# Macaron layer on one core: one more expert measured on ScalarE, four more tiles copied on GpSimd, and the order of all engines redrawn

## What is computed

```python
def ffn(x):                                  # 8 experts of 341 units, 4 chosen, one shared expert
    gate = x @ Wg.T + routing_bias
    weights = softmax(top_4_of(gate))
    out = swiglu(x, Ws1, Ws2, Ws3)           # sigmoid(h) * h * v, h = x @ W1.T, v = x @ W2.T
    for e in range(8):
        out += weights[..., e] * swiglu(x, W1[e], W2[e], W3[e])
    return out

x = x + 0.5 * ffn(layernorm(x))
x = x + attention(layernorm(x))              # 16 heads of 64, causal, 512 x 512 scores
x = x + 0.5 * ffn(layernorm(x))
```

## Time and profile before

| | us |
|---|---|
| time before, median of 3 runs (645.97 to 646.34) | 646.28 |
| time of the profiled execution | 646.15 |
| its span, first to last instruction | 644.4 |
| TensorE busy | 633.5 |
| VectorE busy | 593.0 |
| ScalarE busy | 557.1 |
| GpSimd busy | 506.0 |

### The profile page before, as it was taken

The page is one execution under the profiler, slowest core; times in us unless marked ns, Lnnn a source line. Parts: engine busy times, 40 slices in busy tenths (PEclk is TensorE's granted clock), DMA queues, the critical chain, the costliest instruction groups (busy, mean ns, idle before and its releaser), DMA issues.

```text
span 644.4 us, 21017 instructions
## 1 busy us (share of the span) xinstructions
PE 633.5 (98%) x7872; PEld 418.4 (65%) x7872; DVE 593.0 (92%) x1654; ACT 557.1 (86%) x1080; POOL 506.0 (79%) x633
## 2 busy tenths in 40 slices
PE   7899999999999999999999999999999999999998
PEld 5576655656676566667657666756666676766665
DVE  4999799999999999999999999999999998779887
ACT  4788997999999899999989999988999996475645
POOL 4476596789998878999877899969789997475555
PEclk9999999999999999999999999999999999999999
DMA  7900000689888376898755888863797695201000
GB/s 199 290 3 2 2 2 2 100 134 131 141 128 145 63 128 120 126 148 129 123 93 103 136 145 128 139 128 68 101 146 150 132 134 85 49 2 24 13 1 18
DMA packets 226489, 62.97 MB, mean 98 GB/s; under 512 B 213202, under 2 KB 225620, under 8 KB 226388
## 3 DMA queue, kind: packets, MB, share of 16 engines
q1 hardware_dynamic: 226388, 61.64, 55.9%
HBM read 7.87 MB, written 1.05 MB: 14 GB/s over the span
## 4 chain that ended last, share of the span: by engine, by line
PE 72%; DVE 18%; issue 4%; ACT 3%; SPq 1%; DMA 1%; DVEq 0%; ACTq 0%
PE bank L1197 21%; PE bank L1199 19%; PE bank L1198 19%; PE bank L1391 7%; DVE probs L1896 4%; PE bank L1354 4%; DVE glu L1800 4%; DVE xs L1835 3%; DVE glu L1805 2%; DVE vl L1611 1%; DVE ql L1611 1%; DVE kl L1611 1%; ACT glu L1534 1%; PE bank L1241 1%; DMA paired<-in_L_ffn_W 1%
## 5 line engine op out<-in xcount | busy, mean ns | idle before, releaser
L1160 POOL TENSOR_TENSOR glul<-glu,gluh 128x512 f16<-128x512 f32 x191 | 218.6, 1160 | 46.3 <-ACT gluh L1558 44.8
L1164 POOL TENSOR_TENSOR paired<-probs,paired 128x512 f16<-128x512 f32 x160 | 184.1, 1162 | 23.3 <-ACT paired L1583 22.6
L1537 ACT ACTIVATE glu<-bank,tanh_scale 128x512 f32<-128x512 f32 x167 | 112.4, 680 | 35.9 <-PE bank L1199 34.4
L1575 ACT ACTIVATE probs<-probs,exp_bias 128x128 f32<-128x128 f32 (+3 forms) x256 | 129.4, 553 | 2.7 <-POOL exp_bias L1172 2.6
L1896 DVE CUSTOM_DVE_ANT_0 probs<-bank,causal,score_scale 128x128 f32<-128x128 f32 (+3 forms) x256 | 126.2, 547 | 1.9 <-PE bank L1391 1.0
L1800 DVE SCALAR_TENSOR_TENSOR glu<-glu,bank 128x512 f32<-128x512 f32 x167 | 113.6, 680 | 11.8 <-ACT glu L1537 11.6
L1197 PE MATMUL bank<-w3h,gluh 128*128 128x128 f16 x696 | 122.1, 219 | 0.0
L1199 PE MATMUL bank<-w3h,glul 128*128 128x128 f16 x696 | 121.9, 219 | 0.0
L1198 PE MATMUL bank<-w3l,gluh 128*128 128x128 f16 x696 | 121.9, 219 | 0.0
L1805 DVE SCALAR_TENSOR_TENSOR glu<-glu,bank 128x512 f32<-128x512 f32 x167 | 114.7, 687 | 5.8
L1558 ACT ACTIVATE gluh<-glu 128x512 f16<-128x512 f32 x179 | 107.1, 621 | 13.2 <-DVE glu L1805 12.9
(11 more groups left out here) (228 smaller groups left out, 1621.9 us busy)
## 6 DMA issues: line engine op xcount, KB each, us to landing
pT<-paired SPq DMA_TRANSPOSE x160, 3.3
attention_raw<-in_L_attn_W_qkv SPq DMA_DIRECT2D x6, 256.0 KB, 5.1
xs<-in_L_attn_inputs SPq DMA_DIRECT2D x4, 256.0 KB, 4.6
vh<-in_L_ffn_W SPq DMA_DIRECT2D x6, 128.0 KB
pT<-in_L_ffn_W SPq DMA_DIRECT2D x6, 128.0 KB
out<-xs SPq DMA_DIRECT2D x3, 256.0 KB, 2.7
raw_more<-in_L_ffn_W SPq DMA_DIRECT2D x4, 128.0 KB
attention_raw<-in_L_attn_W_out SPq DMA_DIRECT2D x2, 256.0 KB, 6.1
```

The source lines that it names most:

```text
L1160: pool.tensor_tensor(glul[pair][:, :], g[:, :], gluh[pair][:, :], ALU.subtract).then_inc(glu_low)
L1164: pool.tensor_tensor(paired[n % PAIRED][:, 1, :], probs[n % PROBS][:, :], paired[n % PAIRED][:, 0, :], ALU.subtract).then_inc(probs_low)
L1537: act.activation(g[:, :], psum[b1.bank][:, :], ACT.Tanh, scale=tanh_scale[:, j:j + 1]).then_inc(tanh_made)
L1575: e = act.activation(pr[:, at:at + (qt + 1) * P], pr[:, at:at + (qt + 1) * P], ACT.Exp, bias=exp_bias[:, gp % 2, qt, head:head + 1], scale ...
```

## The change

Two constants and the four strings of `ORDER`. The steps, their banks and SyncE's queue are the same. Of the strings the diff shows the first line of two; all four are redrawn over their whole length.

```diff
-POOLED = 12
+POOLED = 16
 ...
-ADDED_BY = "VVAAAVVVA"
+ADDED_BY = "VVAAAAVVA"
...
     "tensor": (
-        "FFFFFTFFTBzTGNSgTTNhhGSTTTTTThTdhhddhhGddShdTTTddThhTTdddThGhhSTdTTdddhhRdTdhXhdzTTThdddhTgdhhhhhxdd"
+        "BFFFFTTzFFFTGNSgTTNhhGTTSTTTThTdhhddhhGdTSTTddTdhhhTdThdddGThShTThTddddhRdTTdXhhdzddTThhhTdhghhhdxdd"
...
     "scalar": (
-        "lCBzMMMNPPPPNMPhrhPPPhPPPPhhMMAhhhPPAAAhPPhMMMPAAhPhhsssssssssssssPPsAAAshPhsPPlhshszPPPhWQZshsPWWhh"
+        "lCBzMMMNPPPPPMhNrhPPPPhMPPPhhMAhhAAPPPAhAhhMMMhPPPhAhPhPAAAhPPPssssssssssssssssslhhWszPPPhWhhZPsWshh"
```

More of the change, by code:

```diff
@@ L715 @@
     "gpsimd": (
[L716 to L720, removed]
@@ L721 @@
-        "ssssssfsssssssssssssssssssssssH"
+        "LLnLLLLsfsssssLEELEsLsssssEssnssssWssWssssWWssnWssfYWssWWsssnssssbpbpbppsbppsbbppysbpsppbupsbpsbpppb"
+        "ubsspspppbsspbufbpppsbsppbuppbsspsbsppbnupbsppsbpypbubppsssppsssnsuusbypbpbsppbpppbbssppsbspppbbussp"
+        "spbppubsbppsppbsspbubppsspbpuppbbfspspbnppubpbsypsbpppsbusbspppssspssnsuubsyppbbpssbpspppbsbppbsppbu"
+        "bpspsspbppbubpsppfbsppubpbpspbsppubssbppssbpppbnupbspspbpyspbubppsnppsuysssssbsbupsbppfsbpppbsbppspp"
+        "bssppbbusspppbspbupbsppsbppbsbusppnbspppsbbuppsbspppupbbysspbpppbbssusppppssusssfssusssssnsssyssssss"
@@ L722 @@
+        "sssssssssssssfssssssssssssssssH"
     ),
     "tensor": (
-        "FFFFFTFFTBzTGNSgTTNhhGSTTTTTThTdhhddhhGddShdTTTddThhTTdddThGhhSTdTTdddhhRdTdhXhdzTTThdddhTgdhhhhhxdd"
-        "xdddhhhhhhddxhhxzdddkvvhhvvddhhqkhdqqvhdxqxkhddwwqqhwvhkqhwwwdddqqhwvhwqkwhwwddqqxvghwwxdhkwqwhddwwq"
-        "qhdwwqkdhwwqqhwwddqhwwkwhxqxqhwwhdowwqhddwdqqdhwhwhwwhddhhwwwkvvvhwwvxqxddkhdqqhvhddqkohwwqqhwvhwwdq"
-        "khdwqqxvgxwwhwddqwkhddwdwqqhvhwwwqkhwddwqqhhwwwxqxdkhwdqqwwhhwddqkhwwdwwqqhoqhwwddhqqwhxwwhhwxhdwhdd"
@@ L728 @@
[L728 to L731, removed]
+        "BFFFFTTzFFFTGNSgTTNhhGTTSTTTThTdhhddhhGdTSTTddTdhhhTdThdddGThShTTThddddhRdTTdXhhdzddTThhhTdhghhhdxdd"
@@ new lines @@
+        "xdddhhhdhdhhhxzxhdddkvvhhvvddhhqkhdqqvhdxxqhkddqwqvhwwhkqwwhdddqqwhwvhwqkhwwwddqqxvghwwxhkdwqdwhwwdq"
+        "qhdwqwkwhdwqqhwddwqhkwwwhxqxqdhhwwowqhwdwddwqqhhwdhwwhdhdxwhwwkvvvwwhxqvkhddqqhhvddqdkohwqqwwhvhdqww"
+        "khdwqqxgwvxwwhddwqkhddwwdqqhvhwwwqkhwddwqqhhwwwxqxkdhwdqqwhhwwddqkhdwwwqqhwoqhdwwwqqwdhhxhwwxwhhdhdd"
+        "ddwwwkvvhvwvhwkqdhqqvdxhxqkhgdohwwwqqvhwdqkhwwwddqqhhvwwddqkhwwdwqqhvwhwxqxkwhdwwqqhdwqdwkwhhwdqqwwh"
+        "dwdqkhwwdqqhxwwohwwqxhwddqqwwhhddwwhwdhhhwwkvvhvwwvdqkghdxqxqvddhddhqkhdwoqqwhwvhwwqkhdwdwqqxvhhwwwx"
@@ L732 @@
+        "qkhdwwqqvdwhqkwwhwddqqhwhddwwkqwhdwxqxqdwhwhkqwwhddddqqwhwwhowwqdhwqqwhhdhxgwwwxdhhwhhwdddwwddwhhdxh"
+        "hhhoxddddhhhhhdddhxhxdddddhhhhhhhgddxhxddhdhdhdhhhhhddxhxddhhhhdddhhddxhxdddddhhhhhhddxHxddd6"
     ),
     "scalar": (
-        "lCBzMMMNPPPPNMPhrhPPPhPPPPhhMMAhhhPPAAAhPPhMMMPAAhPhhsssssssssssssPPsAAAshPhsPPlhshszPPPhWQZshsPWWhh"
-        "hssrhshsWsWWshhWhsshhWhslsshhszkvvhhsvvsshshsskheeppsvehpeepkpheepslphsvehpeykpheeppeuhsevphpeskephp"
-        "epssssuverpephehkpepshepuepshepeepkhpseepuhpepssshepkhsepepueshhpepsepepuhlyepepehphssepshhseuhphsks"
@@ L737 @@
[L737 to L741, removed]
@@ L742 @@
-        "shhusshhhhsshhsssshhslhshhyssshshhhhssssrhhhssshhhsshhhssshhhsshhshhssssshhhhshshsshsssH"
+        "lCBzMMMNPPPPPMhNrhPPPPhMPPPhhMAhhAAPPPAhAhhMMMhPPPhAhPhPAAAhPPPssssssssssssssssslhhWszPPPhWhhZPsWshh"
+        "sshhssrsWWWshhhQhsslhhsshWWzhssskvvhhsvvsshhsskheepspvheeppehspkeeplvhepphyepkehseppeushpevphsekphep"
+        "epssueehprvseephpspkshepusesephpepkehpeepshuspepshepkhsepepsehuhpelspephyepsepuephhephsehsspepsshhuk"
+        "vvvshulyvskhepsepephshvepkeeephpspsshevphepepkhepepssuvserheppeskhpeupsephepvhepespksheeppuhsehpespu"
@@ new lines @@
+        "ekpheeppshsepheepkpsehpuephlyespephepepsuehshssehppephshsshsepsukvvhvvhluyksehpsepvhepeskhpepseprhse"
+        "psvehpepkeehppespuhehpvsseepkshpeeppuhesvphepepkehupessphepeepkphehpussseehppseekhppeephsupselphepey"
+        "pheessppuhsephsehepphuhlhykvsvhssvvksssuerhepsphevpheekhpseppepssheepvhpepksheepspsuvheheppepskhepes"
+        "uvpehpsepkhepepsehsuhesppespkheeeppulpshhepsekphepuepyepshhepsepesphespuhehpssheeeppprhhussshsshshhu"
+        "shhssshshhshhslsyhhhsssshhshhhhsshhsssrsshshhhsshhshsshhhshhhsssshhshsssshhhsshhhsshsssH"
@@ L743 @@
     ),
     "vector": (
[L745 to L749, removed]
@@ L750 @@
-        "mmhhgriijhhhhccihichhhDDDDhhhccanchhhhhhcchhhhchhhhgrjcchchhhhhhhhchhhcchhhhhccchhhhhhHcccllllllllll"
-        "lM"
+        "nlMMGzSgPPPPUOrOPGhShPPjhPPUPPhhPcGhhSUPPMMMMMchhhPMPPcGPhhShPUPcnhhRPPXPhchcPPzhhhPPghrhhhjcccnhhQh"
+        "hhhnhczhckvvhhvvchhmkhmmhvcmhkmcmvihhmkihcmmhvihmkihmmgrjvchihmikhmmchimkhimchmimhkhimnmhhicanmichmm"
+        "hhiichhhihkvvivchmkhmmvchvhmkcahmmhvihmikhmmgrjvcihmikhcmmhvhimckhimmhiihmckhmmhnihmckihmmihacmhimmh"
+        "hhicihhhncickvvhvvihmkmhmvhcmkhgrjahmmvhimckhimmhivchmkhimmhvihmcikhmmhcimkihhmmichmkhimnhmianhmchmi"
@@ L752 @@
+        "imhcihhchhihkvvhivvmkgrjmhcmchvhmkhcammihvhmikhmmvhhicmikhmmvchimkhimmhhcnimkhicmmihhmikhcmmchhaimih"
+        "mmhhhiigrjhhhcicihchhhhhanchhhhcchhhhccchDDDDhhhhhhgrjhcchhhhchhhhcchhhhchhhhccchhhhhhHcccMlllllllll"
+        "ll"
     ),
```

## The result

| | before | after |
|---|---|---|
| median of 20 runs each, same chip (us) | 645.97 (645.43 to 647.46) | 647.23 (646.69 to 649.32) |
| profiled execution (us) | 646.15 | 647.55 |
| its span (us) | 644.4 | 645.8 |

The ratio after to before is 1.0019, 95% interval 1.0013 to 1.0025: the change costs 1.26 us, where the forecast said 0.6. That lies at the edge of what was called "within 0.2%", inside the range, and on the side that was forecast. The forecast's 646.9 us is nearer to 647.23 than its 0.6 us is to 1.26, and that is luck: it was added to a median of 646.28 us of three runs, and twenty runs of the kernel before gave 645.97.

What follows compares the result with a forecast made beforehand. TensorE was taken to bound the kernel, running back to back from 32.4 us with the other engines hidden. Terms 0 + 0 + 0.1 + 0.5 + 0 = +0.6 us on the 646.28 us median gave 646.9 us, range 645.6 to 649.0.

Steps and rivals of the forecast that it cites:

- Expert 5's sums: Three activations moved to ScalarE, 1.6 us, fit into 2.87 us idle before expert 3's weight halves: cost 0.
- Sixteen pooled tiles: Four copies move from ScalarE to GpSimd; k 15's low half at 63.7 us, wanted at 64.9: cost 0, cover 1.2 us.
- Rival 1: GpSimd's pooled chain, 54 to 64 us, comes late and holds up VectorE: loss 1.3 to 2.3 us, chance 0.12.
- (a): Two turns between gather and spread fill 0.8 us of idle time, but tile 4 then waits 0.7 us for its bank.
- (b): Tile 7 at 32.4 us still waits for a gate function behind VectorE's unmoved scale chain, so nothing is gained.
- (c): On VectorE the first router's rank precedes the second native tile's multiplication; spread at about 23.0 us, 0.1 us later.
- (d): The 0.7 us wait at 18.6 us ends a chain of load, ScalarE sums and weight halves, whose order stays.
- the third rival: TensorE, idle until about 4.5 us, stays slow up to the second native tile at 16 us: +1 to +2 us, chance 0.05.
- TensorE's own work: Changes between half-rows and full matmuls rise from 174 to 180, at 0.09 us each: +0.5 us on the path.
- Behind 33 us: Banks and halves, followed to about 70 us, keep their covers: 0, with bounds -0.5 and +2 us.
- rival 2: Lost covers in attention: new TensorE waits in each of four sequences add 1.5 to 3 us, chance 0.15.
- Rival 4: Faster: VectorE's hold-up at 29.05 us vanishes, small attention gaps go and form changes are free: 644.9 us, chance 0.06.

Runs made afterwards that it cites:

- constants_on_a: ground_a with only the two changed constants, all engine orders staying old: 648.68 us, ratio 1.0039 to the kernel before.
- ground_b: The changed kernel with its 201 transposing DMAs replaced by plain copies: 647.05 us, ratio 1.0016 to the kernel before.
- merged_on_b: ground_b with TensorE's first fifteen steps in the old order and seven single half-rows steps moved beside others: 649.65 us, ratio 1.0053 to the kernel before.
- ground_a: The kernel before with its 201 transposing DMAs replaced by plain copies: 645.90 us, ratio 0.9996 to the kernel before.
- split_on_a: ground_a with twelve pairs of adjacent half-rows steps on TensorE separated: 657.88 us, ratio 1.0180 to the kernel before.

## Why the prediction was right, and where not

**Expert 5's sums: right.** They ran on ScalarE from 27.28 to 28.80 us, 1.5 us for the 1.6 of the sum, and what was idle time of 2.87 us is now 1.80, where 1.3 had been forecast (timeline of ScalarE after):

```profile
27.28 0.54 ACT L1462 ACTIVATE qh<-raw_more 128x384 f16<-128x384 f32 x1
...
32.07 1.27 ACT L1534 ACTIVATE glu<-bank,silu_scale 128x512 f32<-128x512 f32 x2 [1.80 <-DVE silu_back L1696]
```

The cost on the path was 0. The sentence on what they cost without that idle time ("1.6 us at most") is borne out by constants_on_a, where they stood behind it and the third gather lost 1.0 us.

**Sixteen pooled tiles: the place right, the cover mis-sized.** The timeline of GpSimd after, 53 to 70 us:

```profile
55.99 0.21 POOL L1147 TENSOR_TENSOR route<-route,unscale 128x12 f32<-128x12 f32 x1 [5.26 <-DVE tanh_scale L1702]
56.14 0.61 POOL L1156 CAST gluh<-glu 128x512 f16<-128x512 f32 x1
...
59.87 0.23 POOL L1088 TENSOR_SCALAR neg_mean<-moments 128x4 f32<-128x4 f32 x1
...
62.39 1.16 POOL L1160 TENSOR_TENSOR glul<-glu,gluh 128x512 f16<-128x512 f32 x1
...
64.19 3.43 POOL L1160 TENSOR_TENSOR glul<-glu,gluh 128x512 f16<-128x512 f32 x3
```

The steps took about what the sum says (two tiles 3.7, the arithmetic 1.8, two tiles 3.7), but the share began at 55.99 us, not 54.46. So k 15's low half was ready at 65.36 us instead of 63.7, and TensorE, whose norm turn came at 64.48, began k 15 at 65.59 us. The cover was 0.2 us, not 1.2. The term missed is the share: I took its time from before although VectorE's chain ahead of it had been redrawn. That nothing waited is luck: TensorE was itself 0.7 us late there, and at the forecast's 64.9 us it would have waited 0.5 us for k 15. Rival 1 came much closer than its chance says, and stayed without effect at its own place.

What made the share late begins at the fourth group's spread. The timeline of VectorE after:

```profile
49.65 1.10 DVE L1638 TENSOR_SCALAR spread<-ident,greatest_of 15x15 f32<-15x15 f32 x1
```

GpSimd at that time:

```profile
49.57 1.16 POOL L1160 TENSOR_TENSOR glul<-glu,gluh 128x512 f16<-128x512 f32 x1
```

VectorE before:

```profile
49.48 0.22 DVE L1638 TENSOR_SCALAR spread<-ident,greatest_of 15x15 f32<-15x15 f32 x1
```

GpSimd before:

```profile
49.65 1.16 POOL L1160 TENSOR_TENSOR glul<-glu,gluh 128x512 f16<-128x512 f32 x1
```

Before, VectorE's little instruction started 0.17 us ahead of GpSimd's low half and took 0.22 us. After, it started 0.08 us behind one and ended with it, 0.88 us later (49.65 + 1.10 = 50.75, 49.57 + 1.16 = 50.73); ground_b shows the same pair (49.55 with 1.10, 49.46 with 1.16). So do constants_on_a, in all the old orders, and merged_on_b (49.73 with 1.09, 49.63); in ground_a and split_on_a, as before, VectorE began 0.17 to 0.19 us ahead of GpSimd and took 0.22 us. TensorE's spread, which now stands earlier, waited 0.27 us for it. Behind it VectorE's new order of the scale chain has one multiplication less ahead of the first scales and, ahead of the last ones, that multiplication (0.66 us) and a low half of weights (0.57 us). With the hold-up this makes the share's 1.5 us. The Trainium skill ("SBUF — State Buffer", Who interferes with whom) lists `tensor_scalar` among the VectorE instructions that can take the port shared with GpSimd and says that issue order decides which of the two blocks; these four rows agree. How far ahead is enough they leave open: of the pair at 29 us the second instruction starts 0.03 us ahead of GpSimd's low half (29.58 and 29.61 us before) and still takes 1.20 us. The forecast had used this for that one pair, which is unchanged after (29.48 us, 1.71), and had not looked for new ones. There is a second new one, 0.46 us instead of 0.22 at 36.19 us, for which TensorE did not wait. The first is the one cost of the change of the kind of rival 1, 0.27 us.

**The first 33 us: (a) and (b) right, the sum of +0.1 was too small for this profile.** Tile 4 waited for its bank, as (a) has it, but 0.44 us where 0.7 was forecast, and tile 7 waited for its gate function as before. The fixed distances from tile 2 to tile 4 to tile 7 in all seven profiles confirm that the two turns between gather and spread buy nothing. (c) was right in kind and half in size: the spread came at 23.52 us, 4.49 us behind tile 2, for 4.27 before, so 0.22 us later for the 0.1 forecast; tile 4 did not feel it. What failed is (d), "all of these keep their order". The order was kept, but I had only looked at ScalarE's side of the 18.6 us wait. On VectorE's side, the timeline after:

```profile
15.03 0.17 DVE L1648 TENSOR_SCALAR power<-bank 128x10 f32<-128x10 f32 x1 [1.83 <-PE bank L1231]
...
16.77 0.18 DVE L1761 TENSOR_TENSOR shifted<-first_router,top 128x32 f32<-128x32 f32 x1
16.88 0.57 DVE L1611 SCALAR_TENSOR_TENSOR w1l<-bank,half_scale,w1h 128x341 f16<-128x341 f32 x1
```

The first low half of the weights stands behind the first router's arithmetic, which needs the spread and the gate matmuls of TensorE: tile 2 starts 4.42 us behind the first spread in four of the profiles (after, ground_b, ground_a, split_on_a) and is held by ScalarE in the other three. The spread came at 14.61 us instead of 13.82: 0.55 us of that lie ahead of the native tile, with the weights landed late, and 0.24 in its matmuls, which ran at the lower clock until 13.76 us. That is the third rival, the cold start, in kind, but on the first native tile: the clock was up before the second, where the rival put its price (it also counts two matmuls a tile, and there are four), and tile 2 started at 19.03 us, not 20. Whether the new start causes it or two of two profiles had bad luck is open. The two latest rises of the clock (13.69 and 13.76 us, for 12.24 to 13.21 in four others) and the two longest native tiles (2.78 and 2.84 us, for 1.87 to 2.74) speak for a cause; the late landing is chance, and merged_on_b was as late with the old start. The medians leave little for it. Behind tile 7, less the shorter tail, the profiles give 1.0 us (after against before) and 1.25 us (ground_b against ground_a), and the medians differ by 1.26 and 1.15 us in all, so that the start is worth 0.25 or -0.1 us. The 0.41 us may be for the most part the luck of this one profile. The new start alone on ground_a was not run.

**TensorE's own work: right.** The forecast was 6 changes and +0.5 us; five of them cost +0.48 us in the table above and the sixth 0.10, and two experiments with 24 more and 13 fewer give 0.10 us each. This is the largest term of the loss, and the only one of the sum that experiments have priced.

**Behind 33 us: right.** +0.1 us in single idle times, the largest new one under 0.3 us. But the chance of rival 2 (0.15) may have been low. In split_on_a and merged_on_b, whose orders were changed at twelve and at eight places (the second one in its start too) and not redrawn as a whole, TensorE lost 9 and 4 us in covers. The change lost next to none.

**The sum.** 0.41 (start) + 0.48 (forms) + 0.34 (small matmuls, 0.27 of it the hold-up at 50 us) + 0.29 (small idle times, rest) - 0.11 (tail) = 1.41 us, for the 1.43 between the spans. Forecast were 0.1 + 0.5. Rival 4 did not come: TensorE's waits grew in sum, from 6.9 to 8.1 us.

## What to carry to other kernels

Where one engine runs back to back and the others are hidden, moving work among the others gained nothing here, and the price is in the order that must make room for it: count what the new order makes the bound engine itself do (here each change between full-array and half-rows matmuls, 0.10 us), since nothing hides that. Don't trust local exchanges in such an order, even ones that save time on the bound engine, before the banks and halves behind them are followed: eight of them saved 1.3 us and cost 4.2 us in lost covers. When you compute whether a moved chain still arrives in time, compute the start of the chain anew; a start read from the old trace was 1.5 us off and would have eaten all of the cover had the bound engine not been late itself.

## What the hardware showed that I had not expected

- A change from full-array to half-rows matmuls or back costs 0.10 us of TensorE's time in either direction (2.42 us for 24 more, 1.33 us for 13 fewer).
- A 15x15 VectorE instruction took 1.10 us instead of 0.22 because it began 0.08 us behind a GpSimd instruction: a shift of 0.17 us turned into one of 1.05 us. Of seven profiles four have it behind GpSimd (1.09 to 1.14 us) and three ahead (0.22 us each).
- The same f32 matmul took 592 ns later and up to 1193 ns at 11 to 14 us of the span (in ground_a), the ratio of TensorE's two clock levels, 2.4 and 1.2 GHz. A granted clock that reads full in that stretch is no evidence: the record of it begins only where the clock has risen, at 12.2 to 13.8 us in six profiles. How many of the native tile's four were slow differed between profiles with one and the same start (1.87 to 2.74 us for the four). The Trainium skill ("TensorE: Matmul & The Clock Gate", Part 1) says that the moment at which the clock rises varies from run to run; these profiles agree.
- The first raw weights landed 2.9 to 4.0 us after the issue of their last load, with nothing different ahead of them in the queue.
